# A hybrid attention network on one core: projection a chunk ahead, layer norm batch by batch before the convolution, part of the solve's turning on GpSimd, and the first u handed over inside SBUF

## What is computed

```python
# a: 16 heads of 8 channels; q_c, k_c are q, k less their mean over the head
cov  = einsum('bhqd,bhkd->bhqk', q_c, k_c) / d
var  = einsum('bhqo,bhko->bhqk', q_var, k_var) / d        # variances of each token and head
out  = softmax(cov + var) @ v ;  x = x + out @ Wo.T
# b, on the layer-normed x
q = l2norm(conv_silu(silu(x @ Wq.T + bq)))                # k the same; v without the l2norm
a, beta = sigmoid(x @ Wa.T + ba), sigmoid(x @ Wb.T + bb)  # one number for each token and head
S_new = a*S - a*beta*outer(S k, k) + beta*outer(v, k) ;  o = q @ S_new
x = x + o @ Wo.T + bo
# moe: softmax router, top 2 of 8 experts, (silu(x w1) * (x w3)) w2
```

## Time and profile before

| | |
|---|---|
| time, median of 3 runs | 1794.92 us (1792.75 to 1795.29) |
| the profiled execution's own time | 1795.34 us |
| its span, first to last instruction | 1793.6 us |
| PE busy | 1410.8 us (79%) |
| DVE busy | 1418.5 us (79%) |
| ACT busy | 1011.2 us (56%) |
| POOL busy | 328.8 us (18%) |
| mean granted clock of TensorE | 0.887 |

### The profile page before, as it was taken

How to read it: one execution, slowest core, us unless ns; L and a number is a source line. 1 busy time by engine, 2 the same in 40 slices (tenths; PEclk the granted TensorE clock), 3 DMA queues, 4 the chain that set the end, 5 groups by cost and what they waited for, 6 DMA issues and landing times. The chain is left out here.

```text
span 1793.6 us, 43052 instructions
## 1 busy us (share of the span) xinstructions
PE 1410.8 (79%) x16208; PEld 856.8 (48%) x16208; DVE 1418.5 (79%) x2732; ACT 1011.2 (56%) x2101; POOL 328.8 (18%) x471
## 2 busy tenths in 40 slices
PE   4689999999999999999799949783000049969998
PEld 2215555545555555546489915541000014435897
DVE  4678999989899999973756558898999989866564
ACT  3618888888888888886546647612322210014564
POOL 6100000000001100000523500000000026545045
PEclk9959999999999999999899967797555579988999
DMA  3521111111111110002121237225312110011222
GB/s 97 171 69 31 34 33 33 33 33 33 33 32 33 33 33 3 3 3 72 71 65 15 27 79 176 56 47 157 108 47 66 42 53 0 1 38 41 63 19 25
DMA packets 88189, 90.06 MB, mean 50 GB/s; under 512 B 20496, under 2 KB 71632, under 8 KB 87472
## 3 DMA queue, kind: packets, MB, share of 16 engines
q1 hardware_dynamic: 73648, 77.27, 16.7%
q0 software_dynamic: 9856, 7.81, 3.0%
q10 hardware_dynamic: 4480, 2.23, 0.5%
HBM read 46.49 MB, written 29.84 MB: 43 GB/s over the span
## 5 line engine op out<-in xcount | busy, mean ns | idle before, releaser
L724 DVE TENSOR_REDUCE att_negmax<-att_ps_max 128x1 f32<-128x1024 f32 x512 | 621.4, 1223 | 75.0 <-PE att_ps_max L594 46.9
L712 ACT ACTIVATE att_probs<-att_ps_prob 128x512 f32<-128x512 f32 x1024 | 556.4, 595 | 136.4 <-PE att_ps_prob L609 133.1
L594 PE MATMUL att_ps_max<-av_k_op,av_q_op 81*32 81x512 bf16 x4096 | 414.6, 394 | 10.8 <-PEq L104 7.2
L609 PE MATMUL att_ps_prob<-av_q_op,av_k_op 99*32 99x512 bf16 x4096 | 408.4, 383 | 2.4 <-DMA av_q_op<-att_nm_parts 0.8
L626 PE MATMUL att_ps_acc<-att_probs,att_vq 128*32 128x256 f32 x4096 | 314.1, 379 | 0.0
L2284 PE MATMUL out_ps_k<-b_k,b_slots 128*128 128x512 f32 x128 | 62.4, 613 | 238.0 <-PEq L104 231.5
L1175 PE MATMUL moe_moe_ps_up<-moe_moe_xgT,moe_moe_wbuf 128*128 x1328 | 178.4, 278 | 0.0
L594 PEld LDWEIGHTS att_ps_max<-av_k_op,av_q_op 81*32 81x32 bf16 x4096 | 113.5, 97 | 131.6 <-DVE att_negmax L724 28.2
L609 PEld LDWEIGHTS att_ps_prob<-av_q_op,av_k_op 99*32 99x32 bf16 x4096 | 109.5, 95 | 138.9 <-ACT att_probs L712 78.9
L626 PEld LDWEIGHTS att_ps_acc<-att_probs,att_vq 128*32 128x32 f32 x4096 | 131.1, 111 | 81.0 <-issue 1.0
L1175 PEld LDWEIGHTS moe_moe_ps_up<-moe_moe_xgT,moe_moe_wbuf 128*128 128x128 f32 x1328 | 164.5, 195 | 0.2
(11 more groups left out here) (297 smaller groups left out, 1938.8 us busy)
## 6 DMA issues: line engine op xcount, KB each, us to landing
av_k_op<-terms_k SPq DMA_DIRECT2D x48, 216.0 KB
av_q_op<-terms_q SPq DMA_DIRECT2D x144, 72.0 KB
solve_dec_and_windows<-b_k_lane SPq DMA_DIRECT2D x16, 256.0 KB, 4.6
solve_dec_and_windows<-solve_Xw SPq DMA_DIRECT2D x16, 256.0 KB, 3.6
terms_q<-qkv_parts_q SPq DMA_DIRECT2D x8, 384.0 KB, 2.6
terms_k<-qkv_parts_k SPq DMA_DIRECT2D x8, 384.0 KB, 3.1
all_w_all<-in_f_w SPq DMA_DIRECT2D x24, 128.0 KB, 2.4
all_x<-in_a_x ACTq DMA_DIRECT2D x4, 512.0 KB, 7.5
```

What stands on the lines that cost most here:

```text
L594: mm = pe.matmul(ps_max[c * STRIP:(c + 1) * STRIP, n % 2, k * CH:(k + 1) * CH], q_op[s][0:R_ALL, qt // CT, h, at:at + STRIP], k_op[s][0:R_ ...
L609: mm = pe.matmul(ps_prob[c * STRIP:(c + 1) * STRIP, j % 2, :], k_op[s][0:R_END, h, at:at + STRIP], q_op[s][0:R_END, half, h, :], start=Tru ...
L712: act.activation(probs[:, j % PROBS, :], ps_prob[:, j % 2, :], ACT.Exp).then_inc(s_exp, 1)
L724: dve.tensor_reduce(negmax[:, w % 2, a:a + 1], ps_max[:, n % 2, :], AX.X, ALU.max, negate=True).then_inc(s_maxed, 1)
```

## The change

In the projection, turn and projection of chunk c+1 now stand ahead of the variances of chunk c on PE, the copy of xnT stands first in DVE's turn, and the splitting of the variances is done a chunk late, with two `ps_var` buffers. Only head group 0 is loaded during the projection (`EARLY = 1`); group 1 is loaded at the start of `attend`, and groups 2 and 3 after the first maxima. The statistics of x leave the end of moe1, and the block `layer_norm_scales` ahead of the convolution is gone: `project_conv` does this work itself, batch 0 first and the other three together, with x loaded back by batch. A Sqrt of one column stands at the block's start and end (`warm`). `sums` of batch b is issued after the turn of batch b+2, and the loops are written out. In the solve, POOL copies turns 0 and 1 of k. The last window's u of batch 0 goes by 8 DMAs straight into SBUF (`u0`, in the gates' tile), and the rest of it to DRAM, which `delta_out` waits for and loads.

```diff
-        ps_var = m.ps("ps_var", [P, CH])
+        ps_var = [m.ps(f"ps_var{p}", [P, CH]) for p in range(2)]
...
+            def variance_part1(i, p):
+                act.wait_ge(s_var[p], i + 1)
+                wait_used(act, s_vst[p], 32 * i)
+                act.activation(vparts[:, p, 0, :], ps_var[p][0:48, :], ACT.Copy).then_inc(s_v1[p], 1)
+            def variance_part2(i, p):
+                act.wait_ge(s_vr[p], i + 1)
+                act.activation(vparts[:, p, 1, :], vrest[:, p, :], ACT.Copy).then_inc(s_v2[p], 1)
             normalise(0, 0)
             def body(i, last):
                 for p in range(2):
                     if not (last and p == 1):
-                        normalise(i + p, 1 - p)
-                    wait_used(act, s_out[p], 16 * NDMA * i)
+                        normalise(*ahead(i, p))
+                    wait_used(act, s_out[p], 32 * i)
                     for w in range(2):
                         act.wait_ge(s_proj[w][p], i + 1)
                         wait_used(act, s_var[p], i)
                         act.activation(square[w][:, p, :], ps_qk[w][p][:, :], ACT.Square).then_inc(s_sq[w][p], 1)
                         act.activation(parts[w][:, p, 0, :], ps_qk[w][p][:, :], ACT.Copy).then_inc(s_p1[w][p], 1)
+                    if not is_first(i, p):
+                        variance_part1(*behind(i, p))
                     for w in range(2):
                         act.wait_ge(s_r[w][p], i + 1)
                         act.activation(parts[w][:, p, 1, :], rest[w][:, p, :], ACT.Copy).then_inc(s_p2[w][p], 1)
-                    act.wait_ge(s_var[p], i + 1)
-                    act.activation(vparts[:, p, 0, :], ps_var[0:48, :], ACT.Copy).then_inc(s_v1[p], 1)
-                    act.wait_ge(s_vr[p], i + 1)
-                    act.activation(vparts[:, p, 1, :], vrest[:, p, :], ACT.Copy).then_inc(s_v2[p], 1)
+                    if not is_first(i, p):
+                        variance_part2(*behind(i, p))
             chunk_pairs(act, body)
+            variance_part1(NC_ // 2 - 1, 1)
+            variance_part2(NC_ // 2 - 1, 1)
...
             turn(0, 0)
+            project(0, 0)
             def body(i, last):
                 for p in range(2):
-                    pe.wait_ge(s_xnT[p], i + 1)
-                    for w in range(2):
-                        wait_used(pe, s_r[w][p], i)
-                        pe.matmul(ps_qk[w][p][:, :], g.wT[:, w, :], xnT[:, p, :], start=True,
-                                  stop=True).then_inc(s_proj[w][p], 1)
-                    wait_used(pe, s_vout[1 - p], i + p)
-                    for t in range(CT):
-                        mm = pe.matmul(ps_v[:, t * P:(t + 1) * P], xnT[:, p, t * P:(t + 1) * P], g.wT[:, 2, :],
-                                       start=True, stop=True)
-                    mm.then_inc(s_v[p], 1)
                     if not (last and p == 1):
-                        turn(i + p, 1 - p)
-                    wait_used(pe, s_vr[1 - p], i + p)
-                    for w in range(2):
-                        pe.wait_ge(s_sq[w][p], i + 1)
-                        mm = pe.matmul(ps_var[0:48, :], g.varsel[:, w, :], square[w][:, p, :],
-                                       start=(w == 0), stop=(w == 1))
-                    mm.then_inc(s_var[p], 1)
+                        turn(*ahead(i, p))
+                        project(*ahead(i, p))
+                    variances(i, p)
             chunk_pairs(pe, body)
...
+            take_turned(0, 0)
             dve.wait_ge(s_ones, 1)
-            take_turned(0, 0)
+            take_v(0, 0)
             def body(i, last):
                 for p in range(2):
+                    if not (last and p == 1):
+                        take_turned(*ahead(i, p))
                     for w in range(2):
                         dve.wait_ge(s_p1[w][p], i + 1)
                         dve.tensor_tensor(rest[w][:, p, :], ps_qk[w][p][:, :], parts[w][:, p, 0, :],
                                           ALU.subtract).then_inc(s_r[w][p], 1)
+                    if not is_first(i, p):
+                        variance_rest(*behind(i, p))
                     if not (last and p == 1):
-                        take_turned(i + p, 1 - p)
-                    dve.wait_ge(s_v[p], i + 1)
-                    for t in range(CT):
-                        ins = dve.tensor_copy(g.v1[:, bass.ds((2 * i + p) * CT + t, 1), :, 0:D],
-                                              ps_v[:, t * P:(t + 1) * P].rearrange("p (h d) -> p h d", h=H))
-                    ins.then_inc(s_vout[p], 1)
+                        take_v(*ahead(i, p))
                     for w in range(2):
                         dve.wait_ge(s_p2[w][p], i + 1)
                         dve.tensor_tensor(parts[w][:, p, 2, :], rest[w][:, p, :], parts[w][:, p, 1, :],
                                           ALU.subtract).then_inc(s_p3[w][p], 1)
...
+                    if not is_first(i, p):
+                        variance_part3(*behind(i, p))
             chunk_pairs(dve, body)
+            variance_rest(NC_ // 2 - 1, 1)
+            variance_part3(NC_ // 2 - 1, 1)
...
             for c in range(NC_):
                 store(c)
+                if c:
+                    store_variances(c - 1)
...
-EARLY = 2
+                sp.wait_ge(s_out[p], 32 * (NC_ // 2))
+                sp.wait_ge(s_vst[p], 32 * (NC_ // 2))
+EARLY = 1
...
-            for s in range(EARLY, NQ):
+            load(0, 1)
+            max_rows(0)
+            for s in range(2, NQ):
                 load(0, s)
-            max_rows(0)
...
             if norm_next:
-                for i in range(NS // BACK):
-                    some = slice(ND + i * BACK, ND + (i + 1) * BACK)
-                    sp.dma_start(g.x[:, some, :], resid_tiles[:, some, :]).then_inc(s_home[i], 16)
+                for b in range(B):
+                    some = slice(max(ND, b * TB), (b + 1) * TB)
+                    sp.dma_start(g.x[:, some, :], resid_tiles[:, some, :]).then_inc(g.s_home[b], 16)
...
-                for i in range(NS // BACK):
-                    dve.wait_ge(s_home[i], 16)
-                    for t in range(ND + i * BACK, ND + (i + 1) * BACK):
-                        bn_stats_of(nc, g, t)
...
-        def batches(eng, body):
-            body(0, False)
-            with eng.Fori(1, B - 1) as b:
-                body(b, False)
-            body(B - 1, True)
+        def batches(body):
+            for b in range(B):
+                body(b, b == B - 1)
+        groups = [slice(0, TB), slice(TB, NT)]
...
-                        mm = pe.matmul(ps_s[:, CHANNELS[w], bass.ds(b * TB + t, 1)], sq[:, w, t * P:(t + 1) * P], g.ones[:, 0:1],
+                        mm = pe.matmul(ps_s[:, CHANNELS[w], b * TB + t:b * TB + t + 1], sq[:, b % 2, w, t * P:(t + 1) * P], g.ones[:, 0:1],
                                        start=True, stop=True)
                 mm.then_inc(s_sum, 1)
...
             def body(b, last):
                 if not last:
                     turn(b + 1)
+                if b:
+                    sums(b - 1)
+                if not last:
                     project(b + 1)
                     gates(b + 1)
-                sums(b)
-            batches(pe, body)
+            batches(body)
+            sums(B - 1)
...
+            def roots(i):
+                act.wait_ge(s_var, i + 1)
+                act.activation(std[:, groups[i]], var[:, groups[i]], ACT.Sqrt, bias=eps[:, :], scale=1.0 / P
+                               ).then_inc(s_std, 1)
+            act.wait_ge(s_eps, 1)
+            act.activation(warm[:, :], eps[:, :], ACT.Sqrt)
+            roots(0)
+            act.wait_ge(s_ln, 1)
             normalise(0)
+            roots(1)
             act.wait_ge(s_pad, 2)
             for w in range(3):
                 first_silu(0, w)
             def body(b, last):
                 if not last:
+                    act.wait_ge(s_ln, 2)
...
+            act.activation(warm[:, :], eps[:, :], ACT.Sqrt)
...
+            def stats(b):
+                dve.wait_ge(g.s_home[b], 16)
+                for t in range(max(ND, b * TB), (b + 1) * TB):
+                    ins = bn_stats_of(nc, g, t)
+                ins.then_inc(s_stats, 1)
...
+            dve.memset(eps[:, :], LN_EPS).then_inc(s_eps, 1)
+            stats(0)
+            spreads(0)
+            scales(0)
+            stats(1)
             take_turned(0)
+            for b in range(2, B):
+                stats(b)
+            spreads(1)
+            scales(1)
...
+        def hand_over(eng, dh):
+            w = NW - 1
+            for r in range(2):
+                eng.wait_ge(s_step[r], STEP * WB * (w + 1))
+            for r in range(R):
+                eng.dma_start(u0[dh * R + r:P:D, w * W:(w + 1) * W], xv[HALF * dh:HALF * dh + H, w % 2, r, :]
+                              ).then_inc(g.s_u0, 16)
+            for b in range(1, B):
```

(30 more changed lines are left out.)

129 lines of the change are left out of this document (101 added, 28 removed).

## The result

Five runs of the changed kernel have a median of 1781.76 us (1777.03 to 1784.17), five of the kernel before 1794.61 us (1790.01 to 1795.29): a ratio of 0.9933, 95% interval 0.9918 to 0.9949, some 12 us less (12.9 by the medians).

The account below looks back on a forecast made before the run. No engine full; a ring of waits bounds the projection, and moe1 to the convolution is serial. 8.9 + 5.4 + 0 + 2.9 + 0.6 = 17.8 us off 1795.3 gives 1777 us; own range 1773 to 1781, whole range 1768 to 1785.5.

Parts of the forecast that it names:

- the first rival: Convolution: the sums slow it down, 6.59 us beside 4.92 for the same products; total 1782.3 us, chance 0.2.
- last two signs of being wrong: Whole kernel: attention or either moe takes another time than before, or the sum of gains is below 10 us.
- Projection, 8.9 forecast: Projection of q, k, v: a shorter period between xnT copies gains 8.9 us, bounds 5.5 to 10.5.
- The ring: Projection: engines waiting for each other in turn set the period per chunk, 8.03 us before, 6.3 after.
- half clock in the projection: Projection: PE at half clock through the whole stage, 11.1 us per chunk, total 1807 us; chance 0.02.
- Moved loads, 0: Attention: later loads of head groups 1 to 3 stay covered and cost 0.
- moe1 to the convolution, 5.4: Between moe1 and first convolution: normalisation starts 7.7 us earlier, part given back, gain 5.4 us, bounds 3.4 to 7.7.
- Sums a batch late, 0: Convolution: the wait moves from the copy to the first convolution at two batch changes, gain 0.
- Solve's start, 2.9: Start of the solve: hidden Sqrt table load and two turns moved to POOL gain 2.9 us; 1.0 with slow POOL.
- what is late next: Solve's start: after the gains k_scale's DMA is the next wait, and its path gains only 1.28 us.
- Hand-over, 0.6: Solve to delta_out: DVE starts at 1460.7 and not 1461.34, gain 0.6 us, range 0 to 1.5.
- The releaser: Hand-over: DVE's first product in delta_out is released by PE, not by a DMA.

Follow-up runs that it names:

- f_spread: Changed kernel with the early loads spread, one group of four DMAs behind the stores of chunks 2, 3 and 4: 1787.50 us, ratio 0.9926.
- best: Changed kernel with the old hand-over, the early loads spread and batch 2's statistics ahead of the first turned batch's copies: 1781.93 us, ratio 0.9895.
- x_conv: Changed kernel with batch 2's statistics ahead of the first turned batch's copies and sums behind the next batch's gates: 1790.75 us, ratio 0.9955.
- c_after: The changed kernel run once more, nothing edited, beside the kernel before: 1781.32 us, ratio 0.9935.

## Why the prediction was right, and where it was not

The total held: 1781.8 us stands inside 1768 to 1785.5, and the gain is some 12.6 us where 17.8 was forecast. But it stands outside the forecast's own 1773 to 1781, and next to 1782.3, the number of the first rival, whose mechanism did not come: the sums that stand between turn and projection took 4.95 and 4.49 us in the first trace, not 6.59. It held with the projection, the solve and the hand-over short of their terms and 2.1 us of the convolution won that no term had, and that is in part luck. Of its last two signs of being wrong, a sum under 10 us was met on the third chip alone (9.8); the other, another time for attention or a moe, was met in the first trace by moe2 (1.9 us), though not as an effect of the change as far as the traces tell.

**Projection, 8.9 forecast.** The ring was right: 6.1 to 6.4 us against 6.3, and the last third part of the best trace ends at 81.8 against 81.0. The size was not. In nine executions of this projection (three of the changed kernel, six of kernels that differ from it elsewhere) the scores started at 85.0 to 89.5, median 87.8, so 5.2 us are gained and not 8.9; 3.5 to 8.0 over all. The step that failed is the one which left the DMA queue out of the ring: the prediction counted the copies and products of a period of 6.3 us, but not that the store of chunk 3 has to land before chunk 5 overwrites its parts, with eight loads issued just ahead. With the longer period of before there was time for that. `f_spread` shows the cause (the wait falls from 2.9 to 4.3 us to 0.6), and `best`, with the same loads, has no such wait. In five of the nine TensorE's clock also fell, and these have the scores at 87.8 to 89.5 where the other four have 85.0 to 85.9. The rival "half clock in the projection" had the mechanism, and put it in the whole stage; it is one chunk.

**Moved loads, 0.** Right: attention took 734.1 to 735.5 us with them and 735.3 before.

**moe1 to the convolution, 5.4.** Right, by its own steps: 5.45 in the trace, and 14.52 us in every execution in which the statistics were left alone. The normalisation started 9.9 us behind GpSimd's drain start (10 forecast), and ScalarE's second root gave back what was said. What is given back is the order of VectorE's work: one batch of statistics ahead of the copies recovers 1.5 us (`x_conv`, `best`).

**Sums a batch late, 0.** Right, and the trace seemed to say otherwise. The waits moved from the copy to the first convolution of batches 2 and 3, as laid out (1.42 and 0.96 us against 2). The stretch was 2.1 us shorter, and would have been taken for this part's gain; with the order put back it stays short. So the gain belongs to what the other parts change; that it is TensorE's shorter pause ahead of the convolution is argued from its clock and not shown. In the layout the turn was put too late: it ended 7.4 us behind the batch's first convolution and not 8.2, and the batch took 16.6 and 16.1 us where 17.6 was laid out.

**Solve's start, 2.9.** 2.16 in the trace, 0.9 to 2.2 over the executions. GpSimd's turns took 1.07 us each (1.2 estimated). The step that failed is "what is late next": k_scale was named, and ScalarE waits first for the lanes of v, 2.05 us, which SP loads behind the norms' store. The table load: 1.28 us from bias to clamp without the early Sqrt. The rule of the Trainium skill weighed there (ScalarE: Activation LUTs, "What ACT_TABLE_LOAD costs": a drain of 1.38 us besides the load) would have given 2.66; no run here shows the drain: 7.38 less 6.10 is the load alone.

**Hand-over, 0.6.** Wrong in sign: -0.8 to -1.0. The releaser was right (VectorE's product waits for TensorE), but the issue of 7 DMAs was priced at 0.43 each. It took 0.61 to 0.69 for those into scattered partitions, 4.0 us in all for a queue and not 3.0, and the block ends behind it: TensorE starts 5.3 us behind the last reduction, not 4.1.

**Not in the sum: the recurrence, -1.7.** No term spoke of it, since the change leaves it alone. Its loop turns stop VectorE longer where code ahead of it is written out. The stretch around it, from beta's product to the last reduction, has some 1.9 us more in five of the thirteen traces of changed kernels, the second wait for TensorE's sums that `c_after` shows.

The terms as measured, 5.2 + 5.45 + 2.1 + 2.0 - 1.7 - 0.9, make 12.2 us, and the medians of the three measurements of the changed kernel show 12.9, 12.6 and 9.8. The first trace's 18.3 had besides that 1.9 us of moe2, where the one trace of the kernel before is slow, 0.6 of attention, and a projection at the lucky end. What stays open is why the third chip gives 9.8 (its moe1 takes 129.5 us behind its first `wbuf` and up to 130.0 in the other kernels on that chip, where the first trace has 125.8; there is no trace of the kernel before on that chip, so whether it is slower there too is not known).

## What to carry to other kernels

When a ring of engines gets shorter, put the DMA queue into it: for every buffer, ask when its last store must have landed, and what was issued ahead of that store. Spread large transfers over the periods, and neither bunch them nor push them to the end of a block that waits for everything. A DMA added ahead of a block's end costs its issue, and that price is not the same for every DMA: 0.61 us here where 0.43 was assumed. And a gain in a stretch belongs to an edit only once that edit alone has been undone, and against more than one trace of the unedited stretch: here the order of the sums looked worth 2.1 us, and was worth nothing.

## What the runs showed of the hardware

In the projection TensorE idled 1.4 to 2.8 us, made one turn and idled 0.8 us more. In five of nine executions of this code its granted clock then fell to 0.50 to 0.69 (mean of 72 to 76 us), in four it stayed at 1.00. The first pause was 1.69, 1.91, 2.05, 2.14 and 2.75 us where it fell, and 1.42, 1.62, 1.87 and 2.10 us where it stayed, so between 1.7 and 2.1 us its length alone doesn't tell. A loop that nobody touched took 218.7 to 219.1 us in place of 217.2 when code ahead of it was written out, and 217.7 in the one trace in which that was a loop again. DMAs into partitions eight apart took SP 0.61 us to issue, against 0.43 for the old stores to DRAM. And GpSimd turned 128x512 with a stride in 1.07 us, as ScalarE does (1.05).
